# Edge phase 2 of a four-layer graph network: the bias of the scalar outputs on VectorE instead of TensorE, the activation copy one turn later

## The chip, the cores and the metric

The kernel runs on one core of a Trainium2 chip. The metric is the device time of one execution in microseconds (us), and lower is better. Before the change it is 6049.73 us, the median of three runs (6048.89 to 6055.41).

## What is computed

Four graph layers run one after the other on 50,000 nodes (64 scalars and 32 three-vectors each) and 25,000 edges. The change lies in the edge half of the third layer (`L2_gnn`), and only this part of the reference matters. For each edge, the scalars and vectors of both ends are transformed and added (`ms`, `mv`), multiplied by weights `w1` to `w5` that come from a small network of the edge, combined with the edge's direction, and then led through one linear map, whose scalar half has a bias:

```python
def _eq_lin(s, v, ws, bs, wv):
    return (s @ ws + bs, jnp.einsum('nud,uk->nkd', v, wv))
...
ds = jnp.concatenate([o0a, o0b], axis=1)
dv = jnp.concatenate([o1a, o1b, o1c], axis=1)
ls, lv = _eq_lin(ds, dv, lin_ws, lin_bs, lin_wv)
alpha = ls[:, :H * A].reshape(e, H, A)
vs = ls[:, H * A:].reshape(e, H, H0)
vv = lv.reshape(e, H, H1, 3)
a = jnp.einsum('ehk,hk->eh', _smooth_leaky(alpha), alpha_dot)
```

`ls` has 128 columns: 64 go into the smooth leaky activation (here a Silu and a scaled copy), 64 are values. `bs` is `lin_bs`, 128 numbers. The softmax over the edges of a node and all that follows lie in later phases.

## The kernel before

The program is a row of phases with a barrier between them. `edge_phase_23(nc, 2, ...)` is the phase of the change; the same function with `l == 3` serves the fourth layer, where the changed lines are not used. All arithmetic is float32. The 25,000 edges are cut into NB = 49 blocks of B = 512 edges, each block into T = 4 tiles of 128 edges.

Each engine runs its own list of stages through `edge_pipeline`. In turn m of an engine's program a stage `(lag, f)` works on block m - lag, in the order in which the list is written; nothing but this order and the semaphores decides what runs when. Turns 12 to 47 are a hardware loop of four turns a pass, the turns ahead and behind are written out. The lists of `l == 2` are at L1306 (VectorE), L1354 (ScalarE) and L1434 (TensorE). GpSimd only issues eight indirect gathers a block (`gather`, L1162) when the block three ahead has been transposed. SyncE loads indices and stores `val`.

What one turn does, in TensorE's order:

- `weights(0)` (L1400): edge weights of group 0, `ph<-esT,wsb`. `transformed(0)` (L1388): transformed scalars, `pf<-ts,wsb`; it waits until ScalarE has copied two of the three transposed groups `ts` (L1317).
- `outputs(0, 1)` (L1411 to L1414): the linear map of tiles 0 and 1 of the block one older, into `po`. L1413 is the bias: `lead` has ones in row 0 and zeros elsewhere, `ob_2` has the bias in row 0, and the product adds it to the 128 scalar columns.
- `weights(1)`, `transformed(1)` (L1400, L1390, L1391). `transformed(1)` writes the one buffer `pf` again, so it waits until VectorE's `weigh(0)` (L1268) has read it.
- `weights(2)` (L1400), `outputs(2, 3)`, and `turn_rows` (L1379): the transposes of a younger block.

ScalarE copies each finished tile from `po` to `ob` (L1337), the weights from `ph` to `ws` (L1323) and the transposed rows from `pt` to `ts` (L1317). Its stage `silu` has two instructions: the activation `sl` (L1344) and the value copy into `val` (L1346), both of `ob`. VectorE's turn is `messages` (L1284 to L1300, the cross product, the sums and the attention logits from `ob`), `weigh(0)` (L1268), the row preparation of a younger block (L1227 to L1232), `weigh(1)` (L1271), the row preparation of the other end, and `weigh(2)` (L1271, 96 partitions). `messages` begins when ScalarE has copied the fourth tile of its block. The stage waits for the activation only at L1293.

```python
edge_pipeline(v, ((6, messages), (4, weigh(0)), (2, make_rows(0)), (4, weigh(1)), (2, make_rows(1)), (4, weigh(2))))
...
edge_pipeline(a, ((4, weights(0)), (5, outputs(0, 1)), (4, weights(1)), (4, weights(2)), (5, outputs(2, 3)), (5, silu), (3, copies)))
```

Of the kernel before, what the change touches and what calls it, by code (L numbers as in the profile page):

```python
# [19 lines left out]
ALU = mybir.AluOpType  # L20
# [3 lines left out]
P = 128  # L24
# [989 lines left out]
def edge_phase_23(nc, l, x, agg, dram, wt, later, yn):  # L1014
# [16 lines left out]
    with ExitStack() as ctx:  # L1031
# [16 lines left out]
        if l == 3:  # L1048
            tidx = [sb(f"tidx{r}", [P, T], I32) for r in range(R)]
            trow = [sb(f"trow{r}", [P, B], I32) for r in range(R)]  # L1050
            tf = sb("tf", [P, T])
            same = [sb(f"same{u}", [P, T, B]) for u in range(2)]
            product = sb("product", [P, T, B])
            cnt = sb("cnt", [P, T])
            away = sb("away", [P, T])
            cidx = [sb(f"cidx{r}", [P, T], U32) for r in range(R)]
            summed = [sb(f"summed{u}", [P, T, W]) for u in range(2)]
        else:
            comb = [sb(f"comb{u}", [P, T, P]) for u in range(2)]
            lead = sb("lead", [P, P])  # L1060
            sl = sb("sl", [P, T, 64])
            sm = sb("sm", [P, T, 64])
            val = [sb(f"val{u}", [P, T, VW]) for u in range(2)]
            zero = sb("zero", [P, ZS * AW[3]])
# [21 lines left out]
        prod_ok = sem("prod_ok")  # L1086
        o_ps = sem("o_ps")
        ob_ok = sem("ob_ok")
        msg_v = sem("msg_v")
        same_ok = sem("same_ok")  # L1090
        idx_step = sem("idx_step")
# [92 lines left out]
        def _(v):  # L1184
# [3 lines left out]
            for u in range(2):  # L1188
                v.memset(pr[u][96:P, 2, :], 0.0).then_inc(blank, 1)
            if l == 2:  # L1190
                v.memset(lead[:], 0.0).then_inc(blank, 1)
                v.wait_ge(blank, R + 3)
                for r in range(R):
                    v.memset(esT[r][64:65], 1.0).then_inc(blank, 1)
                v.memset(lead[0:1], 1.0).then_inc(blank, 1)
                v.wait_ge(b_ps, 1)
                v.tensor_tensor(wt("mb2"), wt("mb2"), ph[:, 0, 0:1], ALU.add).then_inc(folded, 1)
                v.tensor_scalar(wt("f1_2"), wt("f1_2"), wt("ln1w"), None, ALU.mult).then_inc(folded, 1)
                for s in range(2):
                    v.tensor_scalar(wt(f"f2_2{s}"), wt(f"f2_2{s}"), wt("ln1v"), None, ALU.mult).then_inc(folded, 1)  # L1200
                v.wait_ge(b_ps, 2)
                v.tensor_copy(wt("f1_2"), pf[:, 0:P]).then_inc(folded, 1)
# [9 lines left out]
            def at(y, n, lo, hi):  # L1212
                return y[:, bass.ds(n * T, T), lo:hi].unsqueeze(2).to_broadcast([P, T, V1, hi - lo])

            def c3(a):
                return a.rearrange("p t (u c) -> p t u c", c=3)
# [57 lines left out]
            def messages(i, r, k, parts):  # L1274

                u = r % 2
                o = ob[u]
                vec = o[:, :, VO:VO + V3]
                e = o[:, :, TO:TW].rearrange("p t (u c) -> p t u c", c=5)
                v.wait_ge(ob_ok, T * (i + 1))  # L1280
                v.wait_ge(msg_v, MV * i)
                if l == 2:
                    v.wait_ge(val_ok, 3 * i)
                v.tensor_tensor(c3(m1[:]), e[:, :, :, 1:4], at(ye, i, 2, 5), ALU.mult).then_inc(msg_v, 1)  # L1284
                v.tensor_tensor(c3(m2[:]), e[:, :, :, 2:5], at(ye, i, 1, 4), ALU.mult).then_inc(msg_v, 1)
                v.wait_ge(msg_v, MV * i + 2)
                v.tensor_tensor(m1[:], m1[:], m2[:], ALU.subtract).then_inc(msg_v, 1)
                v.wait_ge(msg_v, MV * i + 3)
                v.tensor_tensor(c3(m2[:]), o[:, :, 0:32].unsqueeze(3).to_broadcast([P, T, V1, 3]), at(yq, i, 0, 3), ALU.mult).then_inc(msg_v, 1)
                v.tensor_tensor(vec, vec, m1[:], ALU.add).then_inc(msg_v, 1)  # L1290
                if l == 2:
                    v.wait_ge(sl_ok, i + 1)
                    v.scalar_tensor_tensor(sm[:], o[:, :, SO:SO + 64], 0.25, sl[:], ALU.mult, ALU.add).then_inc(msg_v, 1)  # L1293
                    v.wait_ge(msg_v, MV * i + 6)
                    v.wait_ge(kept[u], 16 * (2 * k + r // 2))
                    v.tensor_tensor(val[u][:, :, 0:160].rearrange("p t (h k) -> p t h k", h=8)[:, :, :, 8:20], vec.rearrange("p t (h k) -> p t h k", h=8),
                                    m2[:].rearrange("p t (h k) -> p t h k", h=8), ALU.add).then_inc(val_ok, 1)
                    v.tensor_tensor(sm[:], sm[:], wt("adot").unsqueeze(1).to_broadcast([P, T, 64]), ALU.mult).then_inc(val_ok, 1)
                    v.wait_ge(val_ok, 3 * i + 2)
                    v.tensor_reduce(val[u][:, :, 160:168], sm[:].rearrange("p t (h k) -> p t h k", k=8), AX.X, ALU.add).then_inc(val_ok, 1)  # L1300
                else:
                    v.wait_ge(msg_v, MV * i + 5)
                    v.tensor_tensor(vec, vec, m2[:], ALU.add).then_inc(msg_v, 1)
# [6 lines left out]
        @block.scalar  # L1310
        def _(a):
            def copies(i, r, k, parts):
                u = r % 2
                a.wait_ge(f_ps, due(2 * (i - 1)))
                for g in range(NG):
                    a.wait_ge(turned, NG * i + g + 1)
                    a.activation(ts[u][:, g, :], pt[:, g, :], ACT.Copy).then_inc(ts_ok, 1)  # L1317

            def weights(g):
                def f(i, r, k, parts):  # L1320
                    a.wait_ge(w_ps, 3 * i + g + 1)
                    a.wait_ge(prod_ok, 3 * i)
                    a.activation(ws[:, g, :], ph[:, (r + g) % 2 if l == 2 else 0], ACT.Copy).then_inc(w_ok, 1)  # L1323
                return f

            def outputs(*tiles):
                def f(i, r, k, parts):
                    u = r % 2
                    if tiles[0] == 0:
                        if l == 2:  # L1330
                            a.wait_ge(val_ok, due(3 * (i - 1)))
                            a.wait_ge(vs_ok, due(i - 1))
                        else:
                            a.wait_ge(c_ps, due(i - 1))
                    for t in tiles:
                        a.wait_ge(o_ps, T * i + t + 1)
                        a.activation(ob[u][:, t, :], po[:, t % 2, 0:TW], ACT.Copy).then_inc(ob_ok, 1)  # L1337
                return f

            def silu(i, r, k, parts):  # L1340
                u = r % 2
                a.wait_ge(ob_ok, T * (i + 1))
                a.wait_ge(val_ok, 3 * i)
                a.activation(sl[:], ob[u][:, :, SO:SO + 64], ACT.Silu).then_inc(sl_ok, 1)  # L1344
                a.wait_ge(kept[u], 16 * (2 * k + r // 2))
                a.activation(val[u][:, :, 0:160].rearrange("p t (h k) -> p t h k", h=8)[:, :, :, 0:8], ob[u][:, :, SO + 64:SO + 128].rearrange("p t (h k) -> p t h k", h=8), ACT.Copy).then_inc(vs_ok, 1)  # L1346

            def sums(i, r, k, parts):
                a.wait_ge(added, due(16 * T * (i - 1)))
                a.wait_ge(c_ps, i + 1)  # L1350
                a.activation(summed[r % 2][:], pc[:, :, 0:W], ACT.Copy).then_inc(sum_ok, 1)

            if l == 2:
                edge_pipeline(a, ((4, weights(0)), (5, outputs(0, 1)), (4, weights(1)), (4, weights(2)), (5, outputs(2, 3)), (5, silu), (3, copies)))  # L1354
            else:
                edge_pipeline(a, ((4, weights(0)), (5, outputs(0, 1)), (4, weights(1)), (5, outputs(2, 3)), (4, weights(2)), (6, sums), (3, copies)))

        @block.tensor
        def _(pe):
            if l == 2:  # L1360
# [1 line left out]
                pe.wait_ge(folded, 2)  # L1362
                pe.matmul(pf[:, 0:P], wt("centre2"), wt("f1_2"), start=True, stop=True).then_inc(b_ps, 1)
                pe.wait_ge(folded, 5)
                pe.wait_ge(blank, 2 * R + 4)
            else:
                pe.wait_ge(blank, R + 2)

# [34 lines left out]
            def outputs(*tiles):  # L1403
                def f(i, r, k, parts):
                    u = r % 2
                    pe.wait_ge(prod_ok, 3 * i + 3)
                    for t in tiles:
                        pe.wait_ge(ob_ok, due(T * i + t - 1))
                        cut = slice(t * P, (t + 1) * P)
                        if l == 2:  # L1410
                            pe.matmul(po[:, t % 2, 0:TO], pr[u][:, 0, cut], wt("o1_2"), start=True, stop=False)  # L1411
                            pe.matmul(po[:, t % 2, 32:TO], pr[u][:, 1, cut], wt("o2_2"), start=False, stop=False)
                            pe.matmul(po[:, t % 2, BO:TO], lead[:], wt("ob_2"), start=False, stop=True)  # L1413
                            pe.matmul(po[:, t % 2, TO:TW], pr[u][:, 2, cut], wt("o3_2"), start=True, stop=True).then_inc(o_ps, 1)  # L1414
                        else:
                            pe.matmul(po[:, t % 2, 0:TO], pr[u][:, 0, cut], wt("o1_3"), start=True, stop=False)
# [1214 lines left out]
def lay_out(inputs):  # L2631
# [57 lines left out]
    for l in (2, 3):  # L2689
# [21 lines left out]
        put(f"o2_{l}", 96, so - 32, os_[64:96])  # L2711
        for d in range(5):
            put(f"o3_{l}", d % 3, d, ov[96:128], (3, 5))
    put("ob_2", 0, 0, np.reshape(g["L2_gnn_lin_bs"], (1, -1)))
    for h in (0, 64):
        put("h3", h, h, g["L3_gnn_W_fc1"])
    put_rows(3, g["L3_gnn_W_skip0"], g["L3_gnn_W_skip1"])
# [91 lines left out]
```

## Time and profile before

| what | value |
|---|---|
| median of three runs | 6049.73 us |
| profiled execution, its own time | 6039.83 us |
| its span, first to last instruction | 6038.1 us |
| mean granted TensorE clock over the span | 0.929 |
| busy over the span: PE, DVE, ACT, POOL | 86%, 72%, 51%, 64% |
| phase of the change, first to last output product | 2521 to 3108 us |

The profiled execution is 9.9 us (0.16%) under the median of the runs. PE is TensorE's matmuls, PEld its weight loads, DVE is VectorE, ACT is ScalarE, POOL is GpSimd, SP is SyncE. A name such as `L1413 PE MATMUL po<-wsb,lead` gives the line, the engine, the operation, what is written and what is read. Every float32 product here appears as two matmul records. The chain that ended last lies in the last phase, so the phase of the change has to be read by itself, from stretches of it.

### The profile page before, as it was taken

Reading aid. Unit: us, or ns where it says so; the run is one execution under the profiler, and the core shown is the slowest. Engines: PE = TensorE matmul, PEld = TensorE weight load, DVE = VectorE, ACT = ScalarE, POOL = GpSimd, SP = SyncE. Lnnn points to the kernel's source line nnn. Section 1 sums busy time; section 2 is a strip of 40 time slices with the busy share of each in tenths; the row PEclk is TensorE's granted clock in tenths of the full one; section 3 lists DMA queues with packets and bytes.
Section 4 is the critical chain, followed back from the end, with each engine's and each line's share of the span. In section 5 each row is a group of like instructions: output and inputs, shape, how many; then the busy total and the mean of one; then the engine's idle time right before and its main releaser. Section 6 shows DMA issues by size and latency. Waiting matters only on the chain. (4 is left out here: it accounts for less than half of the span.)

```text
span 6038.1 us, 126869 instructions
## 1 busy us (share of the span) xinstructions
PE 5207.7 (86%) x29532; PEld 4038.8 (67%) x29580; DVE 4336.6 (72%) x15122; ACT 3091.9 (51%) x6650; POOL 3854.7 (64%) x4249
## 2 busy tenths in 40 slices
PE   8898977659999799699978888679999989997776
PEld 6565656655666699577756566568888867776766
DVE  3577759874444488688867777568888877775988
ACT  5333327763444366444444443257777744443766
POOL 8687866656888688776614554556666668885222
PEclk9899989998999899899987777789999999998999
DMA  8577766655666676354533333223333335554665
GB/s 321 137 127 119 123 119 224 221 173 112 133 132 126 174 230 227 119 161 157 162 115 83 88 88 89 70 93 108 114 108 108 114 80 86 87 88 90 228 225 184
DMA packets 547954, 837.00 MB, mean 139 GB/s; under 512 B 200220, under 2 KB 298612, under 8 KB 544436
## 3 DMA queue, kind: packets, MB, share of 16 engines
q1 hardware_dynamic: 397235, 666.91, 35.1%
q0 software_dynamic: 150528, 167.91, 16.5%
q8 instruction: 75, 1.23, 0.1%
q14 instruction: 116, 0.94, 0.1%
HBM read 464.00 MB, written 369.33 MB: 138 GB/s over the span
## 5 line engine op out<-in xcount | busy, mean ns | idle before, releaser
L1162 POOL DMA_INDIRECT xg<-x,gidx x588 | 611.0, 1039 | 243.1 <-issue 169.9
L339 POOL DMA_INDIRECT agg<-summed,cidx x392 | 632.2, 1613 | 201.9 <-issue 113.1
L422 DVE TENSOR_TENSOR pr<-pf,ws 128x512 f32<-128x512 f32 x196 | 135.5, 691 | 463.3 <-PE pf L509 356.4
L1337 ACT ACTIVATE ob<-po 128x416 f32<-128x416 f32 (+1 forms) x392 | 197.7, 504 | 353.9 <-PE po L1414 176.9
L1173 POOL DMA_INDIRECT agg<-summed,cidx x196 | 316.4, 1615 | 77.7 <-issue 57.6
L1822 POOL DMA_INDIRECT old_a<-agg,cidx_a x196 | 188.8, 963 | 262.9 <-DMA agg<-new_a,cidx_a 109.4
L1828 POOL DMA_INDIRECT agg<-new_a,cidx_a x196 | 194.8, 994 | 238.5 <-DVE new_a L1924 183.8
L538 PEld LDWEIGHTS pc<-ob,same 128*128 128x128 f32 x1960 | 276.1, 192 | 81.1 <-issue 81.1
L2112 PE MATMUL pk_n<-wsb,xta_n 128*128 128x192 f32 x784 | 222.7, 368 | 112.0 <-ACT xtb_n L2127 112.0
L2205 POOL TENSOR_TENSOR rs_n<-ve_n,wsb 128x4 f32<-128x4 f32 x98 | 98.8, 1008 | 336.8 <-DVE nm_n L2193 336.8
L1400 PE MATMUL ph<-esT,wsb 128*128 128x512 f32 x588 | 303.0, 597 | 2.4 <-DMA trow<-in_src_r 2.4
L538 PE MATMUL pc<-ob,same 128*128 128x161 f32 x1960 | 299.5, 308 | 5.0 <-ACT summed L476 5.0
L644 PE MATMUL pk_n<-wsb,xta_n 128*128 128x160 f32 x784 | 190.4, 325 | 125.7 <-DVE y_n L699 113.1
L1868 DVE TENSOR_REDUCE top_a<-pm_a 128x8 f32<-128x1024 f32 x196 | 238.8, 1220 | 60.0 <-PE pm_a L2002 59.5
L1271 DVE TENSOR_TENSOR pr<-pf,ws 128x512 f32<-128x512 f32 (+1 forms) x245 | 168.5, 688 | 150.5 <-PE pf L1388 83.0
L516 PE MATMUL ph<-hs,wsb 64*128 64x512 f32 x392 | 231.3, 671 | 46.0 <-ACT ws L463 43.6
L1323 ACT ACTIVATE ws<-ph 128x512 f32<-128x512 f32 x294 | 176.9, 602 | 171.7 <-PE ph L1400 167.8
L470 ACT ACTIVATE ob<-po 128x386 f32<-128x386 f32 x196 | 96.5, 492 | 320.9 <-PE po L526 315.7
L2559 POOL TENSOR_TENSOR rsa_n<-var_n,wsb 128x8 f32<-128x8 f32 x98 | 160.5, 1638 | 152.9 <-DVE var_n L2492 152.9
L2142 ACT ACTIVATE xn_n<-y_n,nr_n,rs_n 128x160 f32<-128x160 f32 x392 | 172.1, 509 | 142.4 <-POOL nr_n L2208 142.4
L324 POOL DMA_INDIRECT xg<-in_x,gidx x196 | 201.1, 1026 | 63.1 <-issue 59.7
L509 PE MATMUL pf<-ts,wsb 128*128 128x512 f32 x392 | 236.1, 686 | 1.1 <-ACT ts L449 1.1
(366 smaller groups left out, 17869.3 us busy)
## 6 DMA issues: line engine op xcount, KB each, us to landing
ar_n<-agg SPq DMA_DIRECT2D x194, 322.0 KB
agg<-zero SPq DMA_DIRECT2D x50, 768.0 KB
ar_n<-agg SPq DMA_DIRECT2D x97, 384.0 KB
agg<-zero SPq DMA_DIRECT2D x50, 704.0 KB
ar_n<-agg SPq DMA_DIRECT2D x97, 352.0 KB
agg<-zero_h SPq DMA_DIRECT2D x25, 1288.0 KB, 5.4
agg<-zero SPq DMA_DIRECT2D x50, 644.0 KB
x<-xn_n SPq DMA_DIRECT2D x97, 324.0 KB, 2.5
```

The source lines that it names most:

```text
L324: pool.indirect_dma_start(xg[r][:, t, :], None, x, bass.IndirectOffsetOnAxis(ap=gidx[r][:, t:t + 1], axis=0)).then_inc(gathered[r], 16)
L339: pool.indirect_dma_start(agg, bass.IndirectOffsetOnAxis(ap=cidx[r][:, t:t + 1], axis=0), summed[u][:, t, :], None, compute_op=ALU.add).th ...
L509: pe.matmul(pf[:], wt(f"f{g + 1}_{l}"), ts[r % 2][:, g, :], start=True, stop=True).then_inc(f_ps, 1)
L516: pe.matmul(ph[:], wt(f"w{g + 1}_{l}"), hs[NH - 1][:], start=True, stop=True).then_inc(w_ps, 1)
L538: last = pe.matmul(pc[:, t, 0:W], same[u][:, s, t * P:(t + 1) * P], ob[u][:, s, 32:32 + W], start=(s == t), stop=(s == T - 1))
L1162: pool.indirect_dma_start(xg[s][r][:, t, 0:XR], None, x, bass.IndirectOffsetOnAxis(ap=gidx[s][r][:, t:t + 1], axis=0)).then_inc(gathered[r ...
L1173: pool.indirect_dma_start(agg, bass.IndirectOffsetOnAxis(ap=cidx[r][:, t:t + 1], axis=0), summed[u][:, t, :], None, compute_op=ALU.add).th ...
L1337: a.activation(ob[u][:, t, :], po[:, t % 2, 0:TW], ACT.Copy).then_inc(ob_ok, 1)
L1400: pe.matmul(ph[:, (r + g) % 2 if l == 2 else 0], wt(f"w{g + 1}_{l}"), esT[r][:], start=True, stop=True).then_inc(w_ps, 1)
L1828: pool.indirect_dma_start(table, bass.IndirectOffsetOnAxis(ap=cidx[r][:, t:t + 1], axis=0), new[r % 2][:, t, :], None).then_inc(sent, 16)
L1868: v.tensor_reduce(top[u][:, t, 0:H], pm[t % 2][:], AX.X, ALU.max).then_inc(top_ok, 1)
L2112: pe.matmul(pk[u][:, t, 0:192], xta[u][:, t * P:(t + 1) * P], wt("na_3"), start=True, stop=False)
```

## The change

The bias product L1413 goes, with the tile `lead`. The bias is laid out in all 128 partitions, and VectorE adds it as the first instruction of `messages` to the 128 scalar columns of all four copied tiles (128 x 512 elements). A new semaphore, `bias_ok`, tells ScalarE of it. ScalarE's stage `silu` waits for that one now, and moves from lag 5, behind `outputs(2, 3)`, to lag 6 at the head of the turn, so it stands behind `copies` of the turn before.

```diff
@@ VectorE, set-up
-                v.memset(lead[:], 0.0).then_inc(blank, 1)
-                v.wait_ge(blank, R + 3)
+                v.wait_ge(blank, R + 2)
                 for r in range(R):
                     v.memset(esT[r][64:65], 1.0).then_inc(blank, 1)
-                v.memset(lead[0:1], 1.0).then_inc(blank, 1)
@@ VectorE, messages
                 if l == 2:
                     v.wait_ge(val_ok, 3 * i)
+                    v.tensor_tensor(o[:, :, SO:SO + 128], o[:, :, SO:SO + 128], wt("ob_2").unsqueeze(1).to_broadcast([P, T, 128]), ALU.add).then_inc(bias_ok, 1)
                 v.tensor_tensor(c3(m1[:]), e[:, :, :, 1:4], at(ye, i, 2, 5), ALU.mult).then_inc(msg_v, 1)
@@ ScalarE, silu
-                a.wait_ge(ob_ok, T * (i + 1))
+                a.wait_ge(bias_ok, i + 1)
                 a.wait_ge(val_ok, 3 * i)
                 a.activation(sl[:], ob[u][:, :, SO:SO + 64], ACT.Silu).then_inc(sl_ok, 1)
@@ ScalarE, order
-                edge_pipeline(a, ((4, weights(0)), (5, outputs(0, 1)), (4, weights(1)), (4, weights(2)), (5, outputs(2, 3)), (5, silu), (3, copies)))
+                edge_pipeline(a, ((6, silu), (4, weights(0)), (5, outputs(0, 1)), (4, weights(1)), (4, weights(2)), (5, outputs(2, 3)), (3, copies)))
@@ TensorE, outputs
                             pe.matmul(po[:, t % 2, 0:TO], pr[u][:, 0, cut], wt("o1_2"), start=True, stop=False)
-                            pe.matmul(po[:, t % 2, 32:TO], pr[u][:, 1, cut], wt("o2_2"), start=False, stop=False)
-                            pe.matmul(po[:, t % 2, BO:TO], lead[:], wt("ob_2"), start=False, stop=True)
+                            pe.matmul(po[:, t % 2, 32:TO], pr[u][:, 1, cut], wt("o2_2"), start=False, stop=True)
                             pe.matmul(po[:, t % 2, TO:TW], pr[u][:, 2, cut], wt("o3_2"), start=True, stop=True).then_inc(o_ps, 1)
```

Three places of the built programs show what moves. From `messages` on, the lines of the changed kernel stand one or two lower than before. REGISTER_ALU and ISA are the engine's own address and count arithmetic, not work on tiles.

The first is VectorE, the head of a turn in the loop. Before:

```order
2009 L1281 REGISTER_ALU
2010 L1283 REGISTER_ALU
2011 L1284 ISA
2012 L1284 TENSOR_TENSOR m_2<-ob_2,ye 128x384
2013 L1285 ISA
2014 L1285 TENSOR_TENSOR m_2<-ob_2,ye 128x384
```

And now:

```order
2015 L1281 REGISTER_ALU
2016 L1282 TENSOR_TENSOR ob_2<-ob_2,wsb 128x4x128
2017 L1283 ISA
2018 L1283 TENSOR_TENSOR m_2<-ob_2,ye 128x384
2019 L1284 ISA
2020 L1284 TENSOR_TENSOR m_2<-ob_2,ye 128x384
```

The bias (L1282) stands ahead of the first product, and the address arithmetic of that product (ISA) now stands behind the bias.

The second is ScalarE, the end of a turn in the loop. Before:

```order
797 L1337 ACTIVATE ob_2<-po 128x416
798 L1336 REGISTER_ALU
799 L1337 ACTIVATE ob_2<-po 128x416
800 L1342 REGISTER_ALU
801 L1343 REGISTER_ALU
802 L1344 ACTIVATE sl<-ob_2 128x256
803 L1345 ISA
804 L1346 ACTIVATE val_2<-ob_2 128x4x8x8
805 L1314 REGISTER_ALU
806 L1316 ISA
807 L1317 ACTIVATE ts_2<-pt 128x512
```

And now:

```order
801 L1336 ACTIVATE ob_2<-po 128x416
802 L1313 REGISTER_ALU
803 L1315 ISA
804 L1316 ACTIVATE ts_2<-pt 128x512
805 L1315 REGISTER_ALU
806 L1316 ACTIVATE ts_2<-pt 128x512
807 L1315 REGISTER_ALU
808 L1316 ACTIVATE ts_2<-pt 128x512
809 L1342 REGISTER_ALU
810 L1343 ACTIVATE sl<-ob_2 128x256
811 L1345 ACTIVATE val_2<-ob_2 128x4x8x8
812 L1322 ACTIVATE ws<-ph 128x512
```

The three `ts` copies follow the last `ob` copy directly; activation and value copy stand behind them and ahead of the first `ws` copy of the next turn.

The third is TensorE, the last output tile and the first transposes of a turn in the loop. Before:

```order
1594 L1411 MATMUL po<-wsb,pr_2 128x256
1595 L1412 MATMUL po<-wsb,pr_2 128x224
1596 L1413 MATMUL po<-wsb,lead 128x128
1597 L1414 MATMUL po<-wsb,pr_2 128x160
1598 L1375 ISA
1599 L1379 MATMUL pt<-wsb,xg_2 128x128 x4
```

And now:

```order
1563 L1410 MATMUL po<-wsb,pr_2 128x256
1564 L1411 MATMUL po<-wsb,pr_2 128x224
1565 L1412 MATMUL po<-wsb,pr_2 128x160
1566 L1374 ISA
1567 L1378 MATMUL pt<-wsb,xg_2 128x128 x4
```

One product a tile is gone, four a turn; nothing else moved on this engine.

## Rows read from the trace of the kernel before

**Rows 1.** Busy PE, PEld, DVE, ACT, POOL, granted clock: this, a node, the attention phase.

```profile
2720.00:2820.00 100.00, 98.53 (x460) 69.95 (x459) 83.05 (x166) 48.82 (x99) 69.47 (x67) 1.00 0.51 161
1000.00:1100.00 100.00, 69.65 (x541) 64.20 (x539) 89.02 (x406) 72.20 (x205) 59.70 (x201) 1.00 0.69 222
3200.00:3300.00 100.00, 86.29 (x457) 64.23 (x464) 69.82 (x177) 41.52 (x73) 49.65 (x51) 0.75 0.33 89
```

**Rows 2.** One line's instructions, 2540 to 3100 us: count, ns min/median/max, first and last start.

```profile
L1284 DVE TENSOR_TENSOR m<-ob,ye x46: 557/559/563, 2545.7 to 3091.5; 128x384 f32<-128x384 f32 x46
L1284 DVEq FUSED_REGOPS  x36: 75/78/99, 2606.4 to 3031.2; - x36
```

**Rows 3.** Timeline of TensorE over one turn: start, duration, line, count, idle before.

```profile
2811.72 0.60 PE L1379 MATMUL pt<-wsb,xg 128*128 128x128 f32 x4
...
2813.03 1.02 PE L1400 MATMUL ph<-esT,wsb 128*128 128x512 f32 x2
2814.30 1.12 PE L1388 MATMUL pf<-ts,wsb 128*128 128x512 f32 x2 [0.24 <-ACT ts L1317]
2815.26 0.59 PE L1411 MATMUL po<-wsb,pr 128*128 128x256 f32 x2
2815.70 0.54 PE L1412 MATMUL po<-wsb,pr 128*128 128x224 f32 x2
2816.07 0.39 PE L1413 MATMUL po<-wsb,lead 128*128 128x128 f32 x2
2816.29 0.44 PE L1414 MATMUL po<-wsb,pr 128*128 128x160 f32 x2
...
2817.87 1.02 PE L1400 MATMUL ph<-esT,wsb 128*128 128x512 f32 x2
2818.73 1.02 PE L1390 MATMUL pf<-ts,wsb 128*128 128x512 f32 x2
...
2821.31 0.59 PE L1411 MATMUL po<-wsb,pr 128*128 128x256 f32 x2
...
2823.92 0.60 PE L1379 MATMUL pt<-wsb,xg 128*128 128x128 f32 x4
```

**Rows 4.** Timeline of ScalarE at the end of the turn before that one.

```profile
2811.92 0.52 ACT L1337 ACTIVATE ob<-po 128x416 f32<-128x416 f32 x1 [0.79 <-PE po L1414]
2812.55 0.42 ACT L1344 ACTIVATE sl<-ob 128x256 f32<-128x256 f32 x1
2812.88 0.40 ACT L1346 ACTIVATE val<-ob 128x256 f32<-128x256 f32 x1
2813.18 1.55 ACT L1317 ACTIVATE ts<-pt 128x512 f32<-128x512 f32 x3
2814.61 0.61 ACT L1323 ACTIVATE ws<-ph 128x512 f32<-128x512 f32 x1
```

**Rows 5.** Timeline of VectorE, the turn before and the same turn.

```profile
2800.71 0.56 DVE L1284 TENSOR_TENSOR m<-ob,ye 128x384 f32<-128x384 f32 x1 [1.10 <-ACT ob L1337]
...
2805.26 0.74 DVE L1268 SCALAR_TENSOR_TENSOR pr<-pf,wsb,ws 128x512 f32<-128x512 f32 x1
...
2812.78 0.56 DVE L1284 TENSOR_TENSOR m<-ob,ye 128x384 f32<-128x384 f32 x1 [1.03 <-ACT ob L1337]
...
2815.49 0.42 DVE L1293 SCALAR_TENSOR_TENSOR sm<-ob,sl 128x256 f32<-128x256 f32 x1
...
2817.20 0.74 DVE L1268 SCALAR_TENSOR_TENSOR pr<-pf,wsb,ws 128x512 f32<-128x512 f32 x1
2817.86 0.42 DVE L1227 TENSOR_TENSOR comb<-xg 128x256 f32<-128x256 f32 x1
...
2820.65 0.69 DVE L1271 TENSOR_TENSOR pr<-pf,ws 128x512 f32<-128x512 f32 x1 [0.59 <-PE pf L1391]
2821.26 0.42 DVE L1227 TENSOR_TENSOR comb<-xg 128x256 f32<-128x256 f32 x1
...
2823.24 0.68 DVE L1271 TENSOR_TENSOR pr<-pf,ws 96x512 f32<-96x512 f32 x1
```

More of the change, by code:

```diff
@@ L1059, in edge_phase_23 @@
             comb = [sb(f"comb{u}", [P, T, P]) for u in range(2)]
-            lead = sb("lead", [P, P])
             sl = sb("sl", [P, T, 64])
@@ L1088, in edge_phase_23 @@
         ob_ok = sem("ob_ok")
+        bias_ok = sem("bias_ok")
         msg_v = sem("msg_v")
@@ L1364, in _ @@
                 pe.wait_ge(folded, 5)
-                pe.wait_ge(blank, 2 * R + 4)
+                pe.wait_ge(blank, 2 * R + 2)
             else:
@@ L2713, in lay_out @@
             put(f"o3_{l}", d % 3, d, ov[96:128], (3, 5))
-    put("ob_2", 0, 0, np.reshape(g["L2_gnn_lin_bs"], (1, -1)))
+    put("ob_2", 0, 0, np.broadcast_to(np.reshape(g["L2_gnn_lin_bs"], (1, -1)), (P, 128)))
     for h in (0, 64):
```

## The prediction

> **What bounds the kernel now.** I read the busy times by stretch first. In the phase of the change TensorE's matmuls are busy 98.53 of 100 us at a granted clock of 1.00, VectorE 83, GpSimd 69, ScalarE 49 [rows 1]. A busy TensorE can still hide waits, so the second view is one turn as a timeline. The turn is 12.13 us: the first instruction of `messages` starts at 2545.7 us and, 45 turns on, at 3091.5 [rows 2]. In the turn from 2811.72 to 2823.92 (12.20 us, the loop's branch is in it) TensorE stops in one place: `weights(0)` starts at 2813.03 and needs 0.86 us (such a pair takes a third of the 2.58 us from 2818.73 to 2821.31), but `transformed(0)` starts at 2814.30 and not at 2813.89, and its next follows 0.96 us later, 0.10 late [rows 3]. So 0.51 us a turn are a wait for ScalarE's `ts` copies, the rest is TensorE's own work.
>
> Why the copies are late stands on ScalarE: the last `ob` copy ends at 2812.44, activation and value copy hold the engine until 2813.18, and the second of the three `ts` copies ends near 2814.25 (2813.18, plus a third of the way through 1.55 us, plus its own 0.59) [rows 4]. TensorE resumes 0.05 us behind that.
>
> VectorE waits twice, 1.03 us for the last `ob` copy and 0.59 us for `transformed(1)` [rows 5]. It looks comfortable, but it stands in a loop with TensorE that decides this case.
>
> **The change part by part.**
>
> *TensorE, removed.* A bias product takes 0.22 us from its start to that of the next, 2816.07 to 2816.29 [rows 3]. Four a turn: 0.88 us.
>
> *ScalarE, moved.* Activation and value copy (0.63 us, 2812.55 to 2813.18 [rows 4]) no longer stand ahead of the `ts` copies, and with them TensorE's 0.51 us stop goes: the first copy can start near 0.75 us after the transposes begin, the second ends at 1.85, while TensorE is through `weights(0)` only at 2.17 (1.31 of transposes, 0.86). TensorE alone would then need 12.20 - 0.88 - 0.51 = 10.81 us a turn.
>
> *VectorE, added.* The trace has no VectorE instruction with two SBUF inputs and 512 elements. Below it stands the 384 element one (0.56 us, and steady at 557 to 563 ns through the phase, so GpSimd's gathers beside it cost it nothing) [rows 2], above it the full 0.69 us of the 512 element L1271. I take the time from L1271's start to the next one's, 0.61 us (2820.65 to 2821.26) [rows 5]; the same step is 0.61 from 0.69 because a following instruction starts 0.08 us before its forerunner ends.
>
> The Trainium skill, "VectorE: DVE Perf Modes", gives 691 ns for a float32 `tensor_tensor` of 512 elements (section on the TRN2 errata) and says that the next instruction does not start until the pipe has emptied (section on the DRAIN). The first agrees with the duration here, the second does not with these starts; by the page the sum below would be 0.08 us a turn longer.
>
> *VectorE alone.* From 2812.78 to the end of the last L1271 at 2823.92 are 11.14 us, 0.59 of them the wait for `transformed(1)` [rows 5]. That leaves 10.55, and 11.16 with the bias.
>
> *The loop that takes over.* One turn's work passes through three engines. `messages` must precede `weigh(0)`; `weigh(0)` frees `pf` for `transformed(1)`; then come `weights(2)` and `outputs(2, 3)`; ScalarE copies the last tile; and only then can `messages` of the next block start. The bias is in this loop, and only two of the four removed products are. Its length with the change:
>
> - restart of TensorE behind `weigh(0)`: 0.05 for the release and 0.10 for the exposed weight load, both as behind the `ts` copies [rows 3, 4]
> - `transformed(1)` and `weights(2)`: 2.58 (2818.73 to 2821.31) [rows 3]
> - `outputs(2, 3)`: 2.61 (2821.31 to 2823.92) less two bias products, 2.17 [rows 3]
> - end of the last product to the copy's start: 0.20 (2811.72 to 2811.92), and the copy, 0.52 [rows 3, 4]
> - from the copy's end to VectorE's start: 0.34 now (2812.44 to 2812.78). One address instruction of 75 to 78 ns moves behind the bias [rows 2], so 0.26
> - the bias: 0.61
> - first product to `weigh(0)`: 4.55 in one turn, 4.42 in the next; mean 4.49 [rows 5]
> - `weigh(0)`: 0.74
>
> Sum: 11.72 us. The same sum for the kernel before (0.34 for 0.26, no bias, 2.61 for 2.17) is 11.63, half a microsecond under the 12.13 that it takes. The rows agree: `weigh(0)` ended at 2817.94, and TensorE came to `transformed(1)` at 2818.73 [rows 3, 5]. So the loop is not the bound before, and becomes it.
>
> In a turn that starts with the transposes at 0: `ob` copy done at 0.72, bias from 0.98, first product at 1.59, `weigh(0)` from 6.08 to 6.82. TensorE is ready for `transformed(1)` at 1.31 + 0.86 + 0.86 + 2.17 + 0.86 = 6.06, and waits about 0.8 us. What else could be late is not: ScalarE's `ts` copies end by 2.1, so the activation runs from 2.1 to 2.5, and VectorE asks for it at L1293, 2.71 us behind the first product (2812.78 to 2815.49) [rows 5], at 4.3. The first `ws` copy moves from behind the `ts` copies to about 2.8 to 3.4, and is needed at 6.08. `val` is stored as before, from a stage whose end decides, so SyncE's queue sees no new wait; GpSimd's gathers wait for the transposes and have 30% of their time free.
>
> **The sum.** 12.13 - 11.72 = 0.41 us a turn. The 46 turns of the rows give 18.9 us; the last block pays its bias once more in the open, 0.6 us; the first turns of the phase wait for gathers and gain little. 18.5 us of the profiled execution's 6039.83 gives 6021.3; the median of the runs stands 9.9 us higher, so 6049.7 - 18.5 = 6031 us.
>
> **Bounds.** The terms that the trace doesn't fix are the restart, the release, the bias, and which of the two lengths of `messages` holds. At the low end (restart and release 0, bias 0.48, which is the 0.56 of 384 elements less the overlap of 0.08, and 4.42) the loop is 11.1 us: a gain of up to 47 us. At the high end (restart 0.24, the whole idle that L1388's row shows, release 0.34, bias 0.69, 4.55) it is 12.03: a gain of 4. Each is as likely to err one way as the other, and all at one end at once is not likely, so I keep the middle.
>
> **The rivals.**
>
> *No change that shows* (within 0.2%, 12 us, which is about what a measurement of this kernel can tell from none). It needs a turn of 11.87 to 12.39, that is 0.15 us more in the loop than I count. The upper ends of release and bias together are enough. Around 6043 us.
>
> *TensorE stays the bound*, the loop is shorter than I think, or the bias hides: 10.81 us a turn for TensorE, but VectorE at 11.16 stops it first. 0.97 x 46 = 45 us, 6005 us. Against it: each term of the loop is a row of this trace, and 0.5 us would have to be missing.
>
> *The clock falls, and the kernel is slower.* TensorE now stands still about 0.8 us a turn. The granted clock is 1.00 here but 0.75 in the attention phase, with matmuls busy 86% [rows 1]. The loop has 5.05 us of TensorE's work (0.10, 2.58, 2.17, 0.20). At a mean clock of 0.75 they take 6.7, the turn 13.4, and 46 turns cost 58 us more: 6108 us. It decides when the turn passes 12.39, at a mean clock of about 0.88. Against it: in the node phase the clock is 1.00 with matmuls busy only 70% [rows 1], and here 10.8 of 11.7, 92%, would be left.
>
> This is the rule of the Trainium skill, "TensorE: Matmul & The Clock Gate", section on HAM oscillation: matmul bursts with waits between them lose the full rate and pay for getting it back. [...]
>
> *A new wait in place of the old*, activation behind the bias: L1293 would be reached first only if `bias_ok` came 1.8 us later than I put it. I give it nothing of its own.
>
> **How the numbers follow.** My forecast, the loop as the bound and a turn of 11.4 to 11.87: 64%. No change that shows: 20%. VectorE or TensorE as the bound, 11.4 or less: 9%. Slower: 7%. So faster by over 0.2% 0.73, within 0.2% 0.20, slower 0.07. The range reaches from a turn of 11.4 (6016 us) into the upper half of no change, 6044.
>
> **What the changed profile would show.** The turn at 11.7 us, from the first to the last start of the bias; TensorE's stop ahead of `transformed(0)` gone and a new one of about 0.8 us ahead of `transformed(1)`, ended by `weigh(0)`; matmuls busy about 92% at clock 1.00; VectorE's wait for the last `ob` copy down from 1.03 to about 0.56 (11.72 less 11.16); its wait for `transformed(1)` near zero; the activation behind the `ts` copies with no wait. Wrong would be: a bias longer than 0.7 us, a clock under 1.00, L1293 waiting for ScalarE, or a turn that stays at 12.1.

## The result and the profile after

The changed kernel takes 6023.78 us, the median of six runs (6017.88 to 6030.5), against 6049.31 us for the kernel before in six runs (6041.1 to 6055.41). The medians differ by 25.5 us; the ratio is 0.9963, 95% interval 0.9953 to 0.9973: 0.37% faster, or about 22 us. The forecast was 6031 us, 18.5 us less, in a range of 6016 to 6044. The profiled execution took 6022.5 us, 17.3 less than that of before.

The first view is the same stretch of the phase as in [rows 1]: busy PE, PEld, DVE, ACT, POOL, then the granted clock.

```profile
2720.00:2820.00 100.00, 95.17 (x416) 65.73 (x416) 91.00 (x180) 49.91 (x103) 73.64 (x70) 1.00 0.56 173
```

Matmuls went from 98.53 to 95.17 of 100 us, VectorE from 83 to 91, and the clock stayed at 1.00. The length of a turn comes from one line's instructions in a stretch of the loop: first the kernel before, then the changed one.

```profile
L1284 DVE TENSOR_TENSOR m<-ob,ye x37: 557/559/560, 2606.6 to 3043.0; 128x384 f32<-128x384 f32 x37
```

```profile
L1282 DVE TENSOR_TENSOR ob<-ob,wsb x38: 691/692/694, 2609.0 to 3039.7; 128x512 f32<-128x512 f32 x38
```

436.4 us in 36 turns are 12.12 us, 430.7 us in 37 turns are 11.64. Now one turn of TensorE in the changed kernel, which answers to [rows 3].

```profile
2811.44 1.02 PE L1399 MATMUL ph<-esT,wsb 128*128 128x512 f32 x2
2813.00 1.12 PE L1389 MATMUL pf<-ts,wsb 128*128 128x512 f32 x2 [0.54 <-DVE pr L1266]
2813.96 1.02 PE L1390 MATMUL pf<-ts,wsb 128*128 128x512 f32 x2
...
2815.68 0.59 PE L1410 MATMUL po<-wsb,pr 128*128 128x256 f32 x2
...
2817.84 0.60 PE L1378 MATMUL pt<-wsb,xg 128*128 128x128 f32 x4
...
2819.15 1.02 PE L1399 MATMUL ph<-esT,wsb 128*128 128x512 f32 x2
2820.01 1.02 PE L1387 MATMUL pf<-ts,wsb 128*128 128x512 f32 x2
```

The stop ahead of `transformed(0)` is gone: L1387 starts 0.86 us behind L1399. A new one stands ahead of `transformed(1)`: L1399 is through at 2812.30 (2811.44 and 0.86), and L1389 starts at 2813.00, when VectorE's `weigh(0)` (L1266 here) has ended at 2812.94. ScalarE and VectorE beside it, which answer to [rows 4] and [rows 5]:

```profile
2818.04 0.52 ACT L1336 ACTIVATE ob<-po 128x416 f32<-128x416 f32 x1 [0.56 <-PE po L1412]
2818.48 1.58 ACT L1316 ACTIVATE ts<-pt 128x512 f32<-128x512 f32 x3
2819.93 0.43 ACT L1343 ACTIVATE sl<-ob 128x256 f32<-128x256 f32 x1
```

```profile
2812.20 0.74 DVE L1266 SCALAR_TENSOR_TENSOR pr<-pf,wsb,ws 128x512 f32<-128x512 f32 x1
...
2817.61 0.68 DVE L1269 TENSOR_TENSOR pr<-pf,ws 96x512 f32<-96x512 f32 x1
2818.75 0.69 DVE L1282 TENSOR_TENSOR ob<-ob,wsb 128x512 f32<-128x512 f32 x1 [0.47 <-ACT ob L1336]
2819.36 0.55 DVE L1283 TENSOR_TENSOR m<-ob,ye 128x384 f32<-128x384 f32 x1
...
2822.06 0.42 DVE L1292 SCALAR_TENSOR_TENSOR sm<-ob,sl 128x256 f32<-128x256 f32 x1
...
2823.89 0.74 DVE L1266 SCALAR_TENSOR_TENSOR pr<-pf,wsb,ws 128x512 f32<-128x512 f32 x1
```

The forecast loop can be walked through these rows, from the end of `weigh(0)` (2812.20 and 0.74): TensorE at 2813.00, its output tiles from 2815.68 to 2817.84, the copy from 2818.04 to 2818.56, the bias at 2818.75, the first product at 2819.36, `weigh(0)` from 2823.89 to 2824.63. No step of it has slack, and the round takes 11.69 us. The activation starts at 2819.93 without a wait, and L1292 asks for it 1.7 us after its end.

Over the whole phase, the first start of `messages` is at 2532.3 us and the last at 3108.8 in the kernel before (its L1284), 576.5 us; in the changed kernel, by its bias, it is 550.0:

```profile
L1282 DVE TENSOR_TENSOR ob<-ob,wsb x49: 679/692/694, 2540.3 to 3090.3; 128x512 f32<-128x512 f32 x49
```

So the phase is 26.5 us shorter, more than the 18.5 forecast and more than the difference of the two executions. By the profiled executions the other phases together were 9 us longer in the changed kernel; how far such times differ between executions stands in the last section.

### The profile page after: what moved, and what is told of

The parts are those of the page before. It is cut to its first block and busy times, and to the rows that moved or that the text cites. A ratio compares the mean times of both kernels' runs of the same rounds, so it can differ in the third digit from the quotient of the medians.

```text
span 6020.7 us, 126087 instructions
## 1 busy us (share of the span) xinstructions
PE 5164.2 (86%) x29140; PEld 3989.3 (66%) x29188; DVE 4364.7 (72%) x15169; ACT 3088.2 (51%) x6650; POOL 3848.8 (64%) x4249
## 5 line engine op out<-in xcount | busy, mean ns | idle before, releaser
L1399 PE MATMUL ph<-esT,wsb 128*128 128x512 f32 x588 | 303.5, 598 | 2.7 <-DMA trow<-in_src_r 2.7
```

Of the source, the lines that this page charges most:

```text
L1399: pe.matmul(ph[:, (r + g) % 2 if l == 2 else 0], wt(f"w{g + 1}_{l}"), esT[r][:], start=True, stop=True).then_inc(w_ps, 1)
```

## The experiments

The theory: a turn is as long as the longest of three things, TensorE's own work, VectorE's own work, and the loop `messages`, `weigh(0)`, `transformed(1)`, `weights(2)`, `outputs(2, 3)`, last copy. In the changed kernel it is the loop. Where the activation stands ahead of the `ts` copies, in the kernel before and in `e2_bias_only`, a second loop counts too: last copy, activation, value copy, second `ts` copy, `transformed(0)`, and TensorE's work from there to its last output product. Through [rows 3, 4] it makes the 12.20 us from one start of the transposes, 2811.72, to the next, 2823.92; the three things named first stay at 11.7 or less in the kernel before, whose mean turn is 12.12. The rivals: what counts is TensorE's amount of work; or VectorE's amount of work; or the gain is the removed products' alone. "First to last" in the table is from the first to the last start of `messages` (of its bias where there is one), "turn" that of the same line in the loop, from the stretch 2600 to 3050 us. `e3_no_bias` and `e5_zero_01` to `e8_work_behind` ran once each; what is read from them is the length of the phase and of the turn, which repeat to 0.1 us and 0.01 us where a kernel was profiled twice.

| run | what differs | first to last, us | turn, us |
|---|---|---|---|
| before | | 576.5 | 12.12 |
| changed | | 550.0 | 11.64 |
| `e1_move_only` | activation stage moved, bias on TensorE | 555.3 | 11.70 |
| `e2_bias_only` | bias on VectorE, activation stage not moved | 574.2 | 12.13 |
| `e3_no_bias` | changed, bias left out | 527.2 | 11.16 |
| `e4_split` | changed, `weigh(0)` inside `messages` | 513.0 | 10.77 |
| `e5_zero_01` | changed, two more products in `outputs(0, 1)` | 550.3 | 11.64 |
| `e6_zero_23` | changed, two more products in `outputs(2, 3)` | 571.3 | 12.10 |
| `e7_work_ahead` | changed, addition ahead of `weigh(0)` | 559.4 | 11.84 |
| `e8_work_behind` | changed, addition behind `weigh(0)` | 549.9 | 11.63 |
| `e9_split_products` | `e4_split` with the bias on TensorE | 554.3 | 11.68 |
| `e10_split_again` | `e4_split` | 512.9 | 10.78 |
| `e11_after_again` | changed | 550.1 | 11.65 |

### The two halves of the change apart

`e1_move_only`, from the kernel before:

```diff
-edge_pipeline(a, ((4, weights(0)), (5, outputs(0, 1)), (4, weights(1)), (4, weights(2)), (5, outputs(2, 3)), (5, silu), (3, copies)))
+edge_pipeline(a, ((6, silu), (4, weights(0)), (5, outputs(0, 1)), (4, weights(1)), (4, weights(2)), (5, outputs(2, 3)), (3, copies)))
```

> Only ScalarE's stage moves to the head of the next turn; the bias stays four products a block on TensorE. Theory (each kernel is held by the longer of TensorE's own work and the loop messages, weigh(0), transformed(1), outputs(2, 3), last copy): TensorE's 0.51 us stop for the ts copies goes, so TensorE alone needs 12.13 - 0.51 = 11.62 us a turn, and the loop 11.6 (11.65 as measured in the changed kernel, less the bias 0.61, plus 0.12 of release, plus two products 0.44). Turn 11.6 to 11.7, time within 5 us of the changed kernel, so the whole gain without moving the bias. Rival (the removed products carry the gain): the move gives at most a third of it, turn 11.95 or more, time 6040 or more.

Ratio 0.9968 (0.9956 to 0.9979) against the kernel before. The turn is 11.70 us and the phase 21.2 us shorter, of the 26.5 that the whole change gives. Its TensorE:

```profile
2814.18 0.60 PE L1379 MATMUL pt<-wsb,xg 128*128 128x128 f32 x4
2814.62 1.02 PE L1400 MATMUL ph<-esT,wsb 128*128 128x512 f32 x2
2815.48 1.02 PE L1388 MATMUL pf<-ts,wsb 128*128 128x512 f32 x2
```

`transformed(0)` follows without a stop, 0.86 us behind `weights(0)`, and the busy row of the stretch used before has TensorE at work all the time:

```profile
2720.00:2820.00 100.00, 100.00 (x483) 73.25 (x481) 85.65 (x172) 50.87 (x105) 71.94 (x69) 1.00 0.50 158
```

So this kernel is held by TensorE's own work with all four products, and not by the loop through `weigh(0)`, though the two were expected within 0.1 us of each other. The rival that the removed products carry the gain falls: most of the change's gain comes with the moved activation alone.

`e2_bias_only`, from the changed kernel, is the same line turned back, with the wait for `bias_ok` kept:

```diff
-edge_pipeline(a, ((6, silu), (4, weights(0)), (5, outputs(0, 1)), (4, weights(1)), (4, weights(2)), (5, outputs(2, 3)), (3, copies)))
+edge_pipeline(a, ((4, weights(0)), (5, outputs(0, 1)), (4, weights(1)), (4, weights(2)), (5, outputs(2, 3)), (5, silu), (3, copies)))
```

> The bias on VectorE, but activation and value copy stay at the end of the same turn, ahead of the ts copies. Theory: the activation waits for the bias (about 1.7 us after the transposes begin), the second ts copy ends at 3.45, transformed(0) starts at 3.5, TensorE comes to transformed(1) at 7.5 and ends outputs(2, 3) at 12.2. Turn 12.2, time 6049 to 6056, nothing gained from 0.88 us less of products a turn. Rival (TensorE's work is what counts): turn 12.13 - 0.88 = 11.25, time near 6009.

Ratio 0.9996 (0.9984 to 1.0008): nothing gained, with 0.88 us a turn less for TensorE. ScalarE and TensorE of this run:

```profile
2805.51 0.52 ACT L1336 ACTIVATE ob<-po 128x416 f32<-128x416 f32 x1 [0.56 <-PE po L1412]
2806.95 0.42 ACT L1343 ACTIVATE sl<-ob 128x256 f32<-128x256 f32 x1 [0.92 <-DVE ob L1282]
2807.28 0.40 ACT L1345 ACTIVATE val<-ob 128x256 f32<-128x256 f32 x1
2807.58 1.55 ACT L1316 ACTIVATE ts<-pt 128x512 f32<-128x512 f32 x3
```

```profile
2806.62 1.02 PE L1399 MATMUL ph<-esT,wsb 128*128 128x512 f32 x2
2808.70 1.13 PE L1387 MATMUL pf<-ts,wsb 128*128 128x512 f32 x2 [1.05 <-ACT ts L1316]
```

The activation waits 0.92 us for the bias, the `ts` copies queue behind it, and TensorE starts `transformed(0)` 2.08 us behind `weights(0)` instead of 0.86. The saved products come back as a longer stop: this is the second loop, made longer by the bias.

### The bias left out

The kernel leaves out the bias on both engines, so its output is wrong; it is there for its time.

```diff
-                    v.tensor_tensor(o[:, :, SO:SO + 128], o[:, :, SO:SO + 128], wt("ob_2").unsqueeze(1).to_broadcast([P, T, 128]), ALU.add).then_inc(bias_ok, 1)
...
-                a.wait_ge(bias_ok, i + 1)
+                a.wait_ge(ob_ok, T * (i + 1))
```

> The bias is left out of both engines; the activation stage at the head of the next turn as in the changed kernel. Theory: the loop loses the 0.61 us of the bias and gets 0.12 of address arithmetic back, turn 11.65 - 0.49 = 11.16; TensorE alone needs 10.8 and VectorE alone 10.55. TensorE still waits for weigh(0), about 0.35 us. About 22 us less than the changed kernel. Rival (TensorE is the bound): turn 10.8. Rival (something else holds 11.65): no change against the changed kernel.

Turn 11.16 us, phase 22.8 us shorter than the changed kernel's. So the bias costs the loop 0.48 us a turn there, its 0.61 less the address arithmetic that it covers, and neither TensorE alone (10.8) nor anything at 11.65 holds the turn.

### The same work inside and outside the loop

Two products of zeros, `lead` all zero, in one pair of tiles:

```diff
                             pe.matmul(po[:, t % 2, 32:TO], pr[u][:, 1, cut], wt("o2_2"), start=False, stop=t >= 2)
+                            if t < 2:
+                                pe.matmul(po[:, t % 2, BO:TO], lead[:], wt("ob_2"), start=False, stop=True)
```

`e6_zero_23` has the two conditions the other way round.

> The changed kernel with two products of zeros put back on TensorE, of the size of the bias product, in outputs(0, 1) only (they add nothing). 0.44 us more of TensorE's work a turn, outside the loop messages, weigh(0), transformed(1), outputs(2, 3), last copy. Loop theory: TensorE waits for weigh(0) there anyway (0.7 us), so the turn stays at 11.65. Rival (TensorE's amount of work sets the turn): 12.09.

> The same two products of zeros in outputs(2, 3) only, which is inside the loop. Loop theory: turn 11.65 + 0.44 = 12.09. Rival (VectorE's own work, about 11.1 us and unchanged, is the bound): 11.65 to 11.7. Rival (amount of TensorE work): 12.09 as well, but then the run with the products in outputs(0, 1) gives 12.09 too.

In `outputs(0, 1)` they cost nothing (550.3 against 550.0 us), in `outputs(2, 3)` 21.3 us, 0.46 a turn. The busy rows of the two, the first with the products outside the loop:

```profile
2720.00:2820.00 100.00, 98.73 (x444) 68.90 (x443) 91.35 (x182) 49.36 (x101) 76.59 (x73) 1.00 0.55 172
```

```profile
2720.00:2820.00 100.00, 95.22 (x430) 66.54 (x429) 87.72 (x175) 47.38 (x97) 65.90 (x67) 1.00 0.53 166
```

The kernel whose TensorE is busier is the faster one. Busy matmuls at 98.73% did not make TensorE the bound: it could have done without those products and nothing would have come sooner. The Trainium skill, "Perfetto Trace Analysis", section on identifying the most-contended engine, calls matmul busy time a poor measure of how close a kernel is to its roofline (the most that the engine could do), because pipelined matmuls look smaller in a trace. This pair of runs (98.73% and 95.22% busy, the first faster) also shows it a poor measure, but for another reason: it counts work that nothing waits for.

The same on VectorE, one addition of 128 elements a turn into a tile that nobody reads:

```diff
+            def spare(i, r, k, parts):
+                v.wait_ge(spare_ok, i + 1)
+                v.tensor_tensor(spare_out[:], spare_in[:], spare_in[:], ALU.add).then_inc(spare_ok, 1)
...
-                edge_pipeline(v, ((6, messages), (4, weigh(0)), (2, make_rows(0)), (4, weigh(1)), (2, make_rows(1)), (4, weigh(2))))
+                edge_pipeline(v, ((6, messages), (4, spare), (4, weigh(0)), (2, make_rows(0)), (4, weigh(1)), (2, make_rows(1)), (4, weigh(2))))
```

`e8_work_behind` has `(4, spare)` behind `(4, weigh(0))`.

> The changed kernel with one more VectorE addition a turn, 128 elements into a tile that nobody reads (about 0.20 us by the step of 0.33 for 256 and 0.47 for 384 elements), between messages and weigh(0), which is inside the loop. Loop theory: turn 11.85. Rival (TensorE): 11.65.

> The same extra VectorE addition directly behind weigh(0), outside the loop. Loop theory: VectorE's wait for the last copy (0.4 to 0.5 us, 0.21 of it release) takes it up, turn 11.65 to 11.70. Rival (VectorE's amount of work sets the turn): 11.85, the same as with the addition ahead of weigh(0).

Ahead of `weigh(0)` it costs 0.20 us a turn (11.84) and 9.4 us in the phase, behind it nothing (11.63, 549.9 us). In the second the addition sits between two instructions that had followed each other directly, and the wait for the last copy is shorter for it, 0.33 us here against 0.41 to 0.51 in the changed kernel:

```profile
2808.89 0.74 DVE L1270 SCALAR_TENSOR_TENSOR pr<-pf,wsb,ws 128x512 f32<-128x512 f32 x1
2809.55 0.28 DVE L1310 TENSOR_TENSOR spare_out<-spare_in 128x128 f32<-128x128 f32 x1
2809.75 0.42 DVE L1229 TENSOR_TENSOR comb<-xg 128x256 f32<-128x256 f32 x1
...
2815.44 0.69 DVE L1286 TENSOR_TENSOR ob<-ob,wsb 128x512 f32<-128x512 f32 x1 [0.33 <-ACT ob L1344]
```

Neither TensorE's nor VectorE's amount of work sets the turn, the place of the work does.

### The loop opened: a faster kernel

`messages` is cut behind its third product, and `weigh(0)` stands in the cut. No work is added or taken away.

```diff
                 v.tensor_tensor(m1[:], m1[:], m2[:], ALU.subtract).then_inc(msg_v, 1)
-                v.wait_ge(msg_v, MV * i + 3)
+            def messages_rest(i, r, k, parts):
+                u = r % 2
+                o = ob[u]
+                vec = o[:, :, VO:VO + V3]
+                v.wait_ge(msg_v, MV * i + 3)
...
-                edge_pipeline(v, ((6, messages), (4, weigh(0)), (2, make_rows(0)), (4, weigh(1)), (2, make_rows(1)), (4, weigh(2))))
+                edge_pipeline(v, ((6, messages), (4, weigh(0)), (6, messages_rest), (2, make_rows(0)), (4, weigh(1)), (2, make_rows(1)), (4, weigh(2))))
```

> The changed kernel with weigh(0) put into the middle of messages, behind its third product (L1286), instead of behind all of it. The work is the same. Theory: the loop is opened, since weigh(0) then runs about 3.4 us after the transposes begin and TensorE comes to transformed(1) at 6.06; VectorE's own work, 11.16 us, becomes the bound, TensorE needs 10.8. Turn 11.2, 20 us under the changed kernel, about 6003. Rival (VectorE or a further wait holds the changed kernel): turn stays at 11.6, time within 3 us of it.

5987.18 us, ratio 0.9878 (0.9862 to 0.9895) against the kernel before. The phase is 37.0 us shorter than the changed kernel's; 20 were expected. Its busy row, and VectorE over one turn:

```profile
2720.00:2820.00 100.00, 100.00 (x453) 71.95 (x452) 96.04 (x196) 55.92 (x113) 77.44 (x75) 1.00 0.59 184
```

```profile
2808.81 0.68 DVE L1282 TENSOR_TENSOR ob<-ob,wsb 128x512 f32<-128x512 f32 x1
...
2810.46 0.56 DVE L1286 TENSOR_TENSOR m<-m 128x384 f32<-128x384 f32 x1
2810.93 0.75 DVE L1266 SCALAR_TENSOR_TENSOR pr<-pf,wsb,ws 128x512 f32<-128x512 f32 x1
2811.59 0.55 DVE L1294 TENSOR_TENSOR m<-ob,yq 128x384 f32<-128x384 f32 x1
...
2819.64 0.68 DVE L1282 TENSOR_TENSOR ob<-ob,wsb 128x512 f32<-128x512 f32 x1
```

TensorE has no idle stretch left, and VectorE waits for no other engine: the two now need the same, 10.77 us a turn. The loop was the bound, as expected, but VectorE's own work in this order was overrated by 0.4 us. Most of that is in two places: `weigh(0)` now stands where VectorE had waited for its own result (L1286 and L1288 start 0.71 us apart in the changed kernel, while a step of that size takes 0.47), and I had counted the last instruction's overlap of 0.08 as work.

`e9_split_products` is the same with the bias as products on TensorE; it and two repeats ran on one chip.

> weigh(0) in the middle of messages and the activation stage at the head of the next turn, but the bias still as four products a block on TensorE (0.88 us a turn). Theory: with the loop opened each engine's own work decides, so TensorE's 10.79 + 0.88 = 11.67 is the bound, and the turn is that of the run that only moves the activation; the bias on VectorE is then worth 0.88 us a turn, about 40 us, while it was worth under 0.1 with the loop closed. Rival (the split alone gives the gain of the split kernel): turn near 10.8.

> The split kernel with the bias on VectorE once more, beside the former on one chip: turn 10.79, TensorE without an idle stretch, VectorE at 96%, some 40 us under the kernel with the products.

> The changed kernel again on the same chip: turn 11.65, phase 609 to 610 us, 37 us over the split kernel's phase, and 24 to 27 us under that of the kernel before.

With the products the turn is 11.68, that of the run that only moves the activation, and the ratio 0.9968 (0.9957 to 0.9979); without them 10.78 and 0.9908 (0.9892 to 0.9925); the changed kernel again gave 0.9972 (0.9959 to 0.9985). So the split alone gives nothing over the moved activation, and moving the bias is worth 41.4 us of phase once the loop is open (554.3 less 512.9), where it was worth 5.3 in the closed one (555.3 less 550.0). The whole times are coarser: `e4_split` and `e10_split_again` are the same kernel, with the same phase within 0.1 us, and gave 0.9878 and 0.9908.

## Why the prediction was right

- *What bounds before*: TensorE's own work plus the stop for the `ts` copies. Shown: with the copies moved earlier (`e1_move_only`) the turn is 0.42 us shorter and TensorE's matmuls have no stop. The stop had been read as 0.51, from a turn in which TensorE sat idle 0.24 us ahead of L1388. Over the stretch 2600 to 3060 us of the kernel before, that idle time is 6.9 us in 38 turns, 0.18 each, so the mean stop is nearer 0.45. The row gives the total, the times and the longest:

```profile
PE pf L1388 <- ACT ts L1317: 6.9, 38, 0.2
```

- *The loop takes over, 11.72 us*: 11.64 measured. The turn in the hardware loop is 0.08 shorter than the sum. Release was put at 0.26 and is 0.19 (2818.56 to 2818.75); the bias at 0.61 and is 0.61; restart and the rest as read. Each of the two extra loads placed in the loop shows at its full size, each outside it at nothing.
- *TensorE waits about 0.8 us ahead of `transformed(1)`*: 0.70 in the turn shown.
- *Matmuls busy about 92%*: 95.17% in the profile. The forecast divided TensorE's work by the turn. The profile's busy time counts each product to its end, and the next one starts before that: the pair at 2819.15 lasts 1.02 us and the next starts after 0.86. So 100 less this share is less than the time lost.
- *VectorE's wait for the last copy falls to 0.56*: 0.41 to 0.51. *L1293 doesn't wait*: so it is.
- *The clock stays*: 1.00 in the stretch shown, with this stop in every turn, and 1.00 also in `e2_bias_only`, whose TensorE sits idle 1.05 us in the turn shown. The slower rival did not occur. The section of the Trainium skill that the prediction names for it ("TensorE: Matmul & The Clock Gate", HAM oscillation) describes a kernel whose bursts of matmuls are shorter than the waits between them. Here the stop is 0.7 of 11.6 us, so no run tests that case.
- *The size*: 18.5 us forecast, 26.5 in the phase, about 22 by the ratio of the runs. The forecast applied one saving, 0.41, to 46 turns, and took the first turns to gain little. Of the 26.5 us, 16.8 fall on the 35 steps inside the hardware loop, 5.6 on the six steps ahead of it and 4.1 on the seven behind it, which are written out. 2.0 of the 5.6 are the very first step (13.4 us before, 11.4 in the changed kernel), where gathers may have a part; that was not measured apart. The other written-out turns, too, saved more than those of the loop: in the changed kernel the bias starts at 3051.04 and 3062.46 there, 11.42 us apart, where the kernel before needs 12.1 in this part too. The rows of one such turn, first the last `ob` copy:

```profile
3050.49 0.52 ACT L1336 ACTIVATE ob<-po 128x416 f32<-128x416 f32 x1 [0.56 <-PE po L1412]
```

```profile
3051.04 0.69 DVE L1282 TENSOR_TENSOR ob<-ob,wsb 128x512 f32<-128x512 f32 x1 [0.24 <-ACT ob L1336]
...
3055.95 0.74 DVE L1266 SCALAR_TENSOR_TENSOR pr<-pf,wsb,ws 128x512 f32<-128x512 f32 x1
```

Here the release takes 0.03 us (3051.01 to 3051.04) against 0.19 in the loop, and from the bias to `weigh(0)` it is 4.91 against 5.14 and 5.03. These turns have no address arithmetic between the steps. That this is the cause was not tried apart. So what the forecast had too small is the saving of the turns outside the hardware loop, since all rows that I had used are from inside it; that the time of the runs came out nearer to it than the phase did is owed to the other phases of these executions.
- *VectorE alone, 11.16*: for the order in which it was counted, nearly right. The changed kernel's 11.64 less its wait for the copy (0.41 to 0.51) and the overlap of 0.08 is about 11.1, an estimate from these rows. In the split order it is 10.8. It had no bearing on the forecast turn, since the loop was longer than both.
- *The skill on VectorE*: the prediction quotes the section on the DRAIN of "VectorE: DVE Perf Modes" by half. The same paragraph of the Trainium skill adds that a next instruction which is not held starts earlier, and the starts here, 0.08 us ahead of the end, agree with that. The 0.08 us that the prediction would have added by the page is not what the page asks for.

## What to carry to other kernels

When engines hand work round in a circle within one turn, the turn can be the length of the circle and not the busiest engine's work. Add up each circle, release by release, before costing an edit, and ask of each moved instruction whether it stands on the longest. Where a circle is the bound, work saved beside it is worth nothing, and an instruction that others wait for should stand as early in its engine's list as its inputs allow. Here one line of order (`weigh(0)` ahead of the rest of `messages`) was worth more than the change, and it is what makes moving the bias off TensorE pay.

## What the runs showed of the hardware that was not expected

Executions of one kernel differ by 10 to 28 us here, while the changed phase repeats to 0.1 us (550.0 and 550.1; 513.0 and 512.9). Much of the spread sits in the first edge phase, whose code is the same in all runs. The rows are the first and last start of one of its VectorE lines, in the kernel before, in the changed kernel and in `e10_split_again`.

```profile
L422 DVE TENSOR_TENSOR pr<-pf,ws x98: 682/692/693, 226.5 to 849.3; 128x512 f32<-128x512 f32 x98
```

```profile
L422 DVE TENSOR_TENSOR pr<-pf,ws x98: 677/692/693, 230.9 to 858.3; 128x512 f32<-128x512 f32 x98
```

```profile
L422 DVE TENSOR_TENSOR pr<-pf,ws x98: 682/692/693, 231.6 to 876.2; 128x512 f32<-128x512 f32 x98
```

622.8, 627.4 and 644.6 us for the same work. What makes it slower in some executions was not tried; a single execution's time says little about an edit worth 20 us, the phase's own length does.
